# Position-wise-key attention: scores of two units at once in four row groups, and a new order on three engines

## The chip, the cores and the metric

The kernel runs on one NeuronCore of a Trainium2 chip. The time is the device time of one launch in microseconds (us). Engines are named as in the profile: PE is TensorE's matmul side, PEld its weight load, DVE is VectorE, ACT is ScalarE, POOL is GpSimd. Each engine works its own instructions strictly in the order in which the program lists them, and the engines wait for each other through counting semaphores.

## What is computed

The reference is a decoder of four layers over x (8 rows of 128 tokens, 256 features). The change lies in the self attention of the last layer (`_L3_attn_ref`), whose core is:

```python
x = x + _L3_attn_ref(_layernorm(x), Wq, bq, Wk, bk, Wv, bv, Wo, bo)
H, G = 32, 8; HPG = H // G; HD = 8          # 32 query heads, 8 key heads, 8 features each
q = q.reshape(b, n, H, HD).transpose(0, 2, 1, 3).reshape(b, G, HPG, n, HD)
k = k.reshape(b, n, G, HD).transpose(0, 2, 1, 3)
attn_prob = softmax(einsum('bghnd,bgsd->bghns', q, k) / sqrt(8), axis=-1)
out = einsum('bghns,bgsd->bghnd', attn_prob, v)   # then the product with Wo, plus bo
```

Everything is float32. Before this block comes the feed-forward block of layer 2 (names `L2f_`), behind it the linear cross attention of layer 3 (`L3x_`) and its feed-forward block (`L3f_`).

## The kernel before

**Units.** The block works through the 8 batch rows n. A row has 32 heads, cut into four units of 8 heads, so there are 32 units p = 4n + s. A unit's scores are a tile of 128 queries by 8 x 128 keys (`L3a_S[p % 2]`, two PSUM banks). `L3a_scores(p)` makes it with two matmuls, each over one group of 32 rows of the PE array (`r = 32 * (2 * s % 4 + u)`), with 512 columns; the two matmuls of a unit lie in two different row groups. A unit with even s uses row groups 0 and 1, one with odd s groups 2 and 3, and a half row of heads (c = 0 or 1) is two units.

**A unit's way.** DVE takes the maximum of the scores (`L3a_max`, L3173) and subtracts it into `L3a_P[p % 2]` (`L3a_sub`, L3179); ACT takes the exponential in place (`L3a_exp`, L2032); PE transposes the eight 128 x 128 blocks into the one PSUM tile `L3a_pT` (`L3a_pTr`, L4373); ACT copies that to `L3a_PT[p % 2]` (`L3a_pTc`, L2038). For each two units (a half b = 2n + c) PE multiplies with the values (`L3a_pv`, L4389: four matmuls in four column groups of 32, written to the PSUM bank `L3a_front`), ACT copies (`L3a_oTc`, L2044), PE transposes back into `L3a_oq` (`L3a_oTr`, L4406), and DVE divides by the sum (`L3a_norm`, L3186 and L3190). A row then has `L3a_aoTr` (L4416), the ACT copy `L3a_aoTc` (L2050), `L3a_project` (L4423) and on DVE `L3a_resid` (L3195).

**A row's front.** For the row that comes next: DVE `L3a_stats` and `L3a_u` (L3061), PE `L3a_uTr` (L4260), ACT `L3a_unT`, PE `L3a_value` (L4282) with DVE `L3a_values` (L3075), PE `L3a_qk` (q in L4269, k in L4272, eight matmuls), ACT `L3a_qTc` (L1969, two of them) and DVE `L3a_keys` (L3068, two of them: the keys plus bias, masked for each of four heads, into `L3a_kR`).

**Buffers that are shared.** `L3a_front` is one PSUM bank, used in turn by `uTr`, `qk`, `pv` and `aoTr`, each of which waits until the one before has been copied out. `L3a_oq`, `L3a_v` and `L3a_out` share another bank: `L3a_oTr` therefore waits for `L3a_resid` of the row whose projection lies there. `L3a_pT` is single: a `pTr` waits for the `pTc` before it. `L3a_S`, `L3a_P` and `L3a_PT` are double.

**Order.** Three loops over `p in range(38)`, written out by hand for PE, DVE and ACT, say which of these steps comes when. On PE, scores(p) comes first in each p, and pTr(p - 1) later; scores(p) waits for sub(p - 2), so one unit's scores can be made while DVE still reads those of the unit before.

Of the kernel before, what the change touches and what calls it, by code (L numbers as in the profile page):

```python
# [108 lines left out]
def build_program(nc, dram, out_d):  # L109
# [89 lines left out]
    with stack:  # L199
# [331 lines left out]
        cat = view(sbuf, 45128, [4, 128])  # L531
# [852 lines left out]
        def _(act):  # L1384
# [710 lines left out]

            for p in range(38):
                n, s = p // 4, p % 4
                if 2 <= p < 34:
                    L3a_pTc(p - 2)
                if s == 0 and n < 7:  # L2100
                    L3a_unT(n + 1)
                if s == 2 and n < 7:
                    L3a_qTc(n + 1)
                if s == 3 and n > 0:
                    L3a_aoTc(n - 1)
                if 3 <= p < 34 and p % 2 == 1:
                    L3a_oTc(p // 2 - 1)
                if p < 32:
                    L3a_exp(p)
                if s == 1 and n < 6:  # L2110
                    L3a_rstd(n + 2)
                if p in (29, 30, 31):
                    L3x_rstd(p - 29)
                if p == 32:
                    L3x_kexp(0)
                    L3x_vcopy(0)
                    L3x_unTc(0)
                if p == 34:
                    L3x_qexp(0)
                    L3x_gexp(0)  # L2120
                    L3x_gln(0)
                if p == 35:
                    L3x_kexp(1)
                    L3x_vcopy(1)
                    L3x_unTc(1)
# [112 lines left out]
        def _(dve):  # L2238
# [1005 lines left out]

            for p in range(38):
                n, s = p // 4, p % 4
                if p < 32:
                    L3a_max(p)
                    L3a_sub(p)
                if p == 0:  # L3250
                    L3a_u(1)
                if p == 1:
                    L2f_resid(7)
                if s == 0 and n < 6:
                    L3a_stats(n + 2)
                if s == 1 and n < 7:
                    L3a_values(n + 1)
                if s == 1 and n > 1:
                    L3a_resid(n - 2)
                if 4 <= p < 35 and p % 2 == 0:  # L3260
                    L3a_norm(p // 2 - 2)
                if s == 2 and n < 7:
                    L3a_keys(n + 1)
                if s == 2 and n < 6:
                    L3a_u(n + 2)
                if p == 27:
                    for a in range(2):
                        dve.memset(L3x_v[a][:, :, 128:256], 1.0)
                if p in (28, 29, 30):
                    L3x_stats(p - 28)  # L3270
                if p == 32:
                    L3x_kmin(0)
                if p == 33:
                    L3x_kmap(0)
                    L3x_qmin(0)
                if p == 34:
                    L3x_blocks(0)
                    L3x_qmap(0)
                if p == 35:
                    L3x_kmin(1)  # L3280
                    L3x_kmap(1)

            def L3f_stats(n):
# [119 lines left out]
        def _(pe):  # L3403
# [849 lines left out]
            def L3a_uTr(n):  # L4253
                pe.wait_ge(u_done, L3a_start['u'] + n + 1)
                if n == 1:
                    pe.wait_ge(kTc_done, L3a_start['kTc'] + 1)
                if n > 1:
                    pe.wait_ge(oTc_done, 2 * n - 3)
                for c in range(2):
                    last = pe.transpose(L3a_front[:, 128 * c:128 * c + 128], u0[:, 128 * c:128 * c + 128], ident[:, :])  # L4260
                last.then_inc(uT_done, 1)

            def L3a_qk(n):
                pe.wait_ge(unT_done, L3a_start['unT'] + n + 1)
                if n > 1:
                    pe.wait_ge(oTc_done, 2 * n - 2)
                for j in range(2):
                    for c in range(2):
                        pe.matmul(L3a_front[:, 128 * j:128 * j + 128], w_q3[:, c, 128 * j:128 * j + 128], unT0[:, c, :], start=c == 0, stop=c == 1)  # L4269
                for j in range(2):  # L4270
                    for c in range(2):
                        last = pe.matmul(L3a_front[:, 256 + 128 * j:384 + 128 * j], w_kr3[:, c, 128 * j:128 * j + 128], unT0[:, c, :], start=c == 0, stop=c == 1)  # L4272
                last.then_inc(q_done, 1)

            def L3a_value(n):
                if n > 0:
                    pe.wait_ge(unT_done, L3a_start['unT'] + n + 1)
                    pe.wait_ge(vc_done, L3a_start['vc'] + n)
                if n > 1:
                    pe.wait_ge(norm_done, L3a_start['norm'] + 2 * n - 3)  # L4280
                for c in range(2):
                    last = pe.matmul(L3a_v[:, :], unT0[:, c, :], w_v3[:, c, :], start=c == 0, stop=c == 1)  # L4282
                last.then_inc(v_done, 1)

            def L3a_scores(p):
                n, s = p // 4, p % 4
# [105 lines left out]
            def L3a_oTr(b):  # L4392
# [95 lines left out]
            pe.wait_ge(prod_done, L2f_start['prod'] + 96)  # L4488
            for p in range(38):
                n, s = p // 4, p % 4  # L4490
                if p < 32:
                    L3a_scores(p)
                if p == 0:
                    pe.wait_ge(vc_done, L3a_start['vc'] + 1)
                    L2f_out(7, 0)
                if p == 1:
                    L2f_out(7, 1)
                    pe.wait_ge(resid_done, L2f_start['resid'] + 8)
                if s == 0 and n < 7:
                    L3a_uTr(n + 1)  # L4500
                if 4 <= p < 35 and p % 2 == 0:
                    L3a_oTr(p // 2 - 2)
                if s == 1 and n > 1:
                    L3a_project(n - 2)
                if s == 1 and n < 7:
                    L3a_value(n + 1)
                if s == 2 and n < 7:
                    L3a_qk(n + 1)
                if s == 3 and n > 0:
                    L3a_aoTr(n - 1)  # L4510
                if p == 32:
                    L3x_context(0)
                    L3x_uTr(0)
                if 1 <= p < 33:
                    L3a_pTr(p - 1)
                if p == 33:
                    L3x_qgate(0)
                if 3 <= p < 34 and p % 2 == 1:
                    L3a_pv(p // 2 - 1)
                if p == 33:  # L4520
                    L3x_summary(0)
                if p == 34:
                    L3x_context(1)
                if p == 35:
                    L3x_uTr(1)

            def L3f_uTr(n):
# [290 lines left out]
```

## Time and profile before

| | |
|---|---|
| time, median of 3 | 2115.22 us (2112.89 to 2116.41) |
| the profiled execution: first to last instruction (its span) | 2108.1 us |
| median less that span | 7.1 us |
| first and last score matmul of the block's 32 units start at | 1723.8 and 1855.9 us |
| one period (one row, four units), from unit 8 to unit 28 | 16.29 us |
| busy over the whole span: PE, DVE, ACT, POOL | 87%, 70%, 51%, 52% |
| mean granted TensorE clock | 0.944 of full |

The profile gives only the span of its execution; what the device time counts around the span isn't in it. The block has a steady part, in which each row of four units takes the same 16.29 us, with a start before it (the last products of the block before are mixed in) and an end behind it (the cross attention's first steps are mixed in).

### The profile page before, as it was taken

Reading aid. Unit: us, or ns where it says so; the run is one execution under the profiler, and the core shown is the slowest. Engines: PE = TensorE matmul, PEld = TensorE weight load, DVE = VectorE, ACT = ScalarE, POOL = GpSimd, SP = SyncE. Lnnn points to the kernel's source line nnn. Section 1 sums busy time; section 2 is a strip of 40 time slices with the busy share of each in tenths; the row PEclk is TensorE's granted clock in tenths of the full one; section 3 lists DMA queues with packets and bytes.
Section 4 is the critical chain, followed back from the end, with each engine's and each line's share of the span. In section 5 each row is a group of like instructions: output and inputs, shape, how many; then the busy total and the mean of one; then the engine's idle time right before and its main releaser. Section 6 shows DMA issues by size and latency. Waiting matters only on the chain.

```text
span 2108.1 us, 31396 instructions
## 1 busy us (share of the span) xinstructions
PE 1839.7 (87%) x11498; PEld 1375.0 (65%) x11498; DVE 1485.6 (70%) x2499; ACT 1072.9 (51%) x2328; POOL 1089.3 (52%) x797
## 2 busy tenths in 40 slices
PE   7577779789899987899999999968888789998999
PEld 6111148545689965677777777757777665567887
DVE  5688962466764476677777777589999978866554
ACT  4444431334322254666666666556767656655443
POOL 2599950111692065555555555499999940023321
PEclk9689899689899998999999999989999989999999
DMA  4211001130400000110000000000000001000000
GB/s 162 49 35 35 0 1 40 38 160 0 181 1 1 1 21 21 51 34 1 1 1 1 1 1 17 36 8 1 1 1 1 26 9 74 1 1 1 6 9 9
DMA packets 22177, 54.88 MB, mean 26 GB/s; under 512 B 8591, under 2 KB 13752, under 8 KB 19592
## 3 DMA queue, kind: packets, MB, share of 16 engines
q1 hardware_dynamic: 22024, 52.88, 7.5%
q8 instruction: 92, 1.51, 0.3%
q14 instruction: 61, 0.50, 0.1%
HBM read 44.48 MB, written 1.05 MB: 22 GB/s over the span
## 4 chain that ended last, share of the span: by engine, by line
PE 53%; DVE 19%; POOL 12%; issue 8%; ACT 7%; SPq 1%; DMA 0%; DVEq 0%; POOLq 0%; ACTq 0%
POOL sbuf L1310 5%; PE psum L4153 4%; DVE sbuf L2309 3%; PE psum L4216 3%; PE psum L3507 2%; POOL sbuf L1318 2%; DVE psum L3120 2%; PE psum L4619 1%; POOL sbuf L1111 1%; PE psum L4185 1%; PE psum L4201 1%; PE psum L4157 1%; PE psum L4165 1%; PE psum L4313 1%; ACT sbuf L1893 1%
## 5 line engine op out<-in xcount | busy, mean ns | idle before, releaser
L1310 POOL TENSOR_TENSOR sbuf<-sbuf 128x1035 f32<-128x1035 f32 x128 | 248.4, 1969 | 0.9 <-ACT sbuf L1952 0.9
L4313 PE MATMUL psum<-sbuf 128*128 128x128 f32 (+1 forms) x1024 | 145.3, 292 | 58.4 <-ACT sbuf L1979 42.9
L1979 ACT ACTIVATE sbuf<-sbuf 128x1001 f32<-128x1001 f32 (+1 forms) x128 | 141.9, 1139 | 95.7 <-DVE sbuf L3128 62.9
L4313 PEld LDWEIGHTS psum<-sbuf 128*128 128x128 f32 (+1 forms) x1024 | 126.4, 153 | 79.4 <-ACT sbuf L1979 59.7
L1265 POOL TENSOR_TENSOR sbuf<-sbuf 128x512 f32<-128x512 f32 x64 | 66.7, 1042 | 187.7 <-DVE sbuf L2992 187.7
L1111 POOL TENSOR_TENSOR sbuf<-sbuf 128x1024 f32<-128x1024 f32 x64 | 149.9, 2356 | 16.9 <-DVE sbuf L2309 16.9
L2309 DVE TENSOR_TENSOR_SCAN sbuf<-psum,sbuf 128x1024 f32<-128x1024 f32 x64 | 144.7, 2278 | 12.5 <-ACT psum L1439 6.2
L3455 PE MATMUL psum<-sbuf 96*128 96x512 bf16 x256 | 83.5, 437 | 76.0 <-DVE sbuf L2309 32.7
L1893 ACT ACTIVATE sbuf<-psum,sbuf 128x128 f32<-128x128 f32 x256 | 90.4, 365 | 107.3 <-DVE sbuf L2986 107.3
L1439 ACT ACTIVATE psum<-psum,sbuf 128x1016 f32<-128x1016 f32 x64 | 69.0, 1081 | 125.7 <-PE psum L3455 125.7
L3120 DVE SCALAR_TENSOR_TENSOR psum<-sbuf,psum 128x1024 f32<-128x1024 f32 (+1 forms) x96 | 122.3, 1274 | 9.8 <-PE psum L4303 2.5
L4153 PE MATMUL psum<-sbuf 128*128 128x512 f32 x256 | 123.9, 607 | 3.5 <-POOL sbuf L1261 3.5
L3128 DVE TENSOR_TENSOR sbuf<-psum,sbuf 128x1024 f32<-128x1024 f32 (+1 forms) x96 | 116.4, 1213 | 3.3
L3455 PEld LDWEIGHTS psum<-sbuf 96*128 96x128 bf16 x256 | 18.7, 103 | 153.1 <-DVE sbuf L2309 63.4
L4216 PE MATMUL psum<-sbuf 128*128 128x256 bf16 x768 | 94.6, 273 | 14.5 <-POOL sbuf L1273 14.2
L1271 POOL TENSOR_TENSOR sbuf<-sbuf 128x512 f32<-128x512 bf16 x64 | 74.5, 1164 | 49.7 <-DVE sbuf L3005 48.1
L4216 PEld LDWEIGHTS psum<-sbuf 128*128 128x128 bf16 x768 | 71.3, 98 | 39.9 <-POOL sbuf L1273 30.7
L1363 POOL TENSOR_TENSOR sbuf<-sbuf 128x1024 f32<-128x1024 f32 x16 | 30.8, 1944 | 120.1 <-DVE sbuf L3321 120.1
L2981 DVE TENSOR_TENSOR sbuf<-psum,sbuf 128x512 f32<-128x512 f32 x64 | 44.3, 692 | 57.0 <-ACT sbuf L1877 57.0
L1273 POOL TENSOR_TENSOR sbuf<-sbuf 128x512 bf16<-128x512 f32 x64 | 81.2, 1268 | 5.0
L3486 PE MATMUL psum<-sbuf 128*32 128x512 f32 x256 | 77.6, 738 | 3.9 <-POOL sbuf L1111 3.9
L1099 POOL TENSOR_TENSOR sbuf<-sbuf 128x1024 f32<-128x1024 f32 x22 | 52.2, 2372 | 53.4 <-ACT sbuf L1445 53.4
(808 smaller groups left out, 5105.5 us busy)
## 6 DMA issues: line engine op xcount, KB each, us to landing
sbuf<-sbuf SPq DMA_DIRECT2D x42, 128.0 KB, 2.4
sbuf<-w_p_d SPq DMA_DIRECT2D x8, 512.0 KB, 3.7
sbuf<-w_qkv_d SPq DMA_DIRECT2D x3, 768.0 KB, 4.2
sbuf<-w_e_d SPq DMA_DIRECT2D x1, 2048.0 KB, 7.8
sbuf<-w_gu_d SPq DMA_DIRECT2D x1, 2048.0 KB, 9.0
sbuf<-w_gu_d SPq DMA_DIRECT2D x2, 1024.0 KB, 7.8
sbuf<-w_dn_d SPq DMA_DIRECT2D x1, 2048.0 KB, 15.8
sbuf<-w_q_d SPq DMA_DIRECT2D x1, 2048.0 KB, 8.3
```

The lines of the kernel that those rows point to most:

```text
L1111: pool.tensor_tensor(L0a_hc[i % 4][:, :], L0a_hs[i % 2][:, :], L0a_Cr[g % 4][:, :], ALU.mult).then_inc(hc_done, 1)
L1273: pool.tensor_tensor(cat16[:, :, :], cat[:, :, :], omagic[:, :, :], ALU.subtract).then_inc(cat_done, 1)
L1310: pool.tensor_tensor(P_r[g % 7][:, :, :], rows.unsqueeze(2).to_broadcast([128, 23, 45]), cols.unsqueeze(1).to_broadcast([128, 23, 45]), AL ...
L1893: last = act.activation(prob[:, h, :], L2x_s[:, h, :], ACT.Exp, bias=smax[:, h:h + 1], accum_out=esum[:, h:h + 1])
L1979: act.activation(Q_r[g % 6][:, 0:w], Q_r[g % 6][:, 0:w], ACT.Silu, scale=q8_p[n % 2][:, h:h + 1]).then_inc(silu_done, 1)
L2309: dve.tensor_tensor_scan(L0a_hs[i % 2][:, :], L0a_dAf[i % 2][:, :], L0a_us[i % 3][:, :], 0.0, ALU.mult, ALU.add).then_inc(scan_done, 1)
L3120: dve.scalar_tensor_tensor(M[:, 0:w], Pf_r[g % 7][:, o:o + w], t8_p[n % 2][:, h, 7:8], zps[:, 0:w], ALU.is_ge, ALU.mult).then_inc(mask_don ...
L3128: dve.tensor_tensor(Q_r[g % 6][:, 0:w], Mps[:, 0:w], Pf_r[g % 7][:, o:o + w], ALU.mult).then_inc(prod_done, 1)
L3455: last = pe.matmul(out[:, 512 * h:512 * h + 512], rows, L0a_stack[g % 4][0:96, a, 512 * h:512 * h + 512], start=True, stop=True)
L4153: last = pe.matmul(L2x_q[:, :, :], xs[:, vq, c, :], wq[:, c, 512 * g:512 * g + 512], start=c == 0, stop=c == 1)
L4216: last = pe.matmul(L2x_out[:, :], cat16[:, h, :], w_p3[p][:, 4 * (i % 8) + h, :], start=i % 8 == 0 and h == 0 and p == 0, stop=i % 8 == 7 ...
L4313: last = pe.matmul(Gps[0:m, c, :], Q_r[g % 6][:, 128 * c:128 * c + m], ident[:, :], start=h == 0 and c % 4 == 0, stop=h == 7, skip_group_c ...
```

## The change

The score step takes two units: `L3a_scores(k, units)` issues four matmuls, one in each row group, into both halves of `L3a_S`, and adds one to `score_done` behind each unit's two. It waits for both subtractions of the pair before. The loops run over 19 pair steps k instead of 38 units, and all steps on PE, DVE and ACT are laid into a new order, with the waits that this order needs. Number and shapes of all instructions stay as they are; no buffer is added. POOL's list doesn't change.

```diff
             def L3a_uTr(n):
-                if n == 1:
-                    pe.wait_ge(kTc_done, L3a_start['kTc'] + 1)
-                if n > 1:
-                    pe.wait_ge(oTc_done, 2 * n - 3)
+                if 0 < n < 3:
+                    pe.wait_ge(kTc_done, L3a_start['kTc'] + n)
+                if n > 2:
+                    pe.wait_ge(oTc_done, 2 * n - 4)
...
             def L3a_qk(n):
                 pe.wait_ge(unT_done, L3a_start['unT'] + n + 1)
                 if n > 1:
-                    pe.wait_ge(oTc_done, 2 * n - 2)
+                    pe.wait_ge(oTc_done, 2 * n - 3)
+                if n > 2:
+                    pe.wait_ge(cat_done, L3a_start['cat'] + n - 2)
...
             def L3a_value(n):
-                if n > 1:
-                    pe.wait_ge(norm_done, L3a_start['norm'] + 2 * n - 3)
+                if n > 2:
+                    pe.wait_ge(norm_done, L3a_start['norm'] + 2 * n - 4)
+                if n > 3:
+                    pe.wait_ge(resid_done, L3a_start['resid'] + n - 3)
...
-            def L3a_scores(p):
-                n, s = p // 4, p % 4
+            def L3a_scores(k, units):
+                n, c = k // 2, k % 2
                 pe.wait_ge(kTc_done, L3a_start['kTc'] + n + 1)
-                if p > 1:
-                    pe.wait_ge(sub_done, L3a_start['sub'] + p - 1)
-
-                for u in range(2):
-                    r = 32 * (2 * s % 4 + u)
-                    last = pe.matmul(L3a_S[p % 2][:, 4 * u:4 * u + 4, :], L3a_qT[n % 2][r:r + 32, s // 2, :], L3a_kR[n % 2][r:r + 32, s // 2, :, :], start=True, stop=True)
-
-                last.then_inc(score_done, 1)
+                if k > 0:
+                    pe.wait_ge(sub_done, L3a_start['sub'] + 2 * k)
+                for v in units:
+                    for u in range(2):
+                        r = 32 * (2 * v + u)
+                        last = pe.matmul(L3a_S[v][:, 4 * u:4 * u + 4, :], L3a_qT[n % 2][r:r + 32, c, :], L3a_kR[n % 2][r:r + 32, c, :, :], start=True, stop=True)
+                    last.then_inc(score_done, 1)
...
             def L3a_pv(b):
-                if c == 0 and n < 7:
-                    pe.wait_ge(kTc_done, L3a_start['kTc'] + n + 2)
-                if c == 0 and n > 0:
+                if c == 0 and n < 6:
+                    pe.wait_ge(unT_done, L3a_start['unT'] + n + 3)
+                if c == 1 and n < 6:
+                    pe.wait_ge(kTc_done, L3a_start['kTc'] + n + 3)
+                if c == 1 and n > 0:
                     pe.wait_ge(cat_done, L3a_start['cat'] + n)
-                if c == 1 and n < 6:
-                    pe.wait_ge(unT_done, L3a_start['unT'] + n + 3)
...
             def L3a_oTr(b):
                 if c == 0:
-                    pe.wait_ge(vc_done, L3a_start['vc'] + min(n + 2, 8))
-                if c == 0 and n > 1:
-                    pe.wait_ge(resid_done, L3a_start['resid'] + n - 1)
-                if c == 1:
                     pe.wait_ge(vc_done, L3a_start['vc'] + min(n + 3, 8))
                 if c == 1 and n > 0:
                     pe.wait_ge(resid_done, L3a_start['resid'] + n)
...
             def L3a_aoTr(n):
                 pe.wait_ge(norm_done, L3a_start['norm'] + 2 * n + 2)
-                if n < 6:
-                    pe.wait_ge(kTc_done, L3a_start['kTc'] + n + 3)
-                else:
-                    pe.wait_ge(oTc_done, 2 * n + 2)
+                pe.wait_ge(oTc_done, min(2 * n + 3, 16))
...
             def L3a_project(n):
+                if n < 6:
+                    pe.wait_ge(vc_done, L3a_start['vc'] + min(n + 4, 8))
```

The PE loop after the change (what steps 16 to 18 hold of the cross attention is left out):

```diff
+            for k in range(19):
+                if k == 0:
+                    L3a_scores(0, (0,))
+                    pe.wait_ge(vc_done, L3a_start['vc'] + 1)
+                    L2f_out(7, 0)
+                    L3a_uTr(1)
+                    L3a_scores(0, (1,))
+                    L2f_out(7, 1)
+                    pe.wait_ge(resid_done, L2f_start['resid'] + 8)
+                elif k < 16:
+                    L3a_scores(k, (0, 1))
+                if 1 <= k < 17:
+                    L3a_pTr(2 * k - 2)
+                if 2 <= k < 18:
+                    L3a_pv(k - 2)
+                if k % 2 == 0:
+                    if k < 14:
+                        L3a_value(k // 2 + 1)
...
+                    if k >= 4:
+                        L3a_aoTr(k // 2 - 2)
+                else:
+                    if k >= 5:
+                        L3a_project(k // 2 - 2)
+                    if k < 12:
+                        L3a_uTr(k // 2 + 2)
+                if 2 <= k < 18:
+                    L3a_oTr(k - 2)
+                if 1 <= k < 17:
+                    L3a_pTr(2 * k - 1)
+                if k % 2 == 0 and k < 14:
+                    L3a_qk(k // 2 + 1)
```

The DVE order of step k is now: norm(k - 3), max(2k), sub(2k); with even k then values(k/2 + 1) and u(k/2 + 2), with odd k from 5 on resid((k - 1)/2 - 2); then max(2k + 1), sub(2k + 1); then keys(k/2 + 1) with even k, stats with odd k. The ACT order of step k is: oTc(k - 2), pTc(2k - 2), aoTc (even k) or unT (odd k), exp(2k), pTc(2k - 1), qTc (even k), exp(2k + 1), rstd (odd k). From step 16 on the three loops hold the first steps of the cross attention, as before.

## Rows read from the trace of the kernel before

**Rows 1.** Windows: us, then busy us (and count) of PE, PEld, DVE, ACT, POOL; clock
```profile
1762.00:1843.40 81.40, 75.75 (x504) 46.05 (x500) 66.03 (x94) 51.64 (x78) 2.91 (x4) 1.00 0.00 1
1843.40:1872.40 29.00, 24.99 (x149) 14.68 (x145) 18.02 (x35) 17.56 (x32) 4.38 (x4) 1.00 0.00 1
```

**Rows 2.** Waits, 1774.5 to 1839.7 (four periods): us in total, times, longest
```profile
DVE sbuf L3173 <- PE psum L4293: 11.3, 12, 1.5
```

**Rows 3.** Timeline of one period: start us, us, engine, line, tile, count
```profile
1785.73 0.41 DVE L3195 TENSOR_TENSOR sbuf<-psum,sbuf 128x256 f32<-128x256 f32 x1
...
1787.48 0.66 PE L4406 MATMUL psum<-sbuf 128*128 128x128 f32 x4
...
1787.98 1.06 PE L4269 MATMUL psum<-sbuf 128*128 128x128 f32 x8
...
1788.86 1.22 DVE L3179 TENSOR_TENSOR sbuf<-psum,sbuf 128x1024 f32<-128x1024 f32 x1
1788.87 1.06 PE L4272 MATMUL psum<-sbuf 128*128 128x128 f32 x8
...
1789.77 1.04 PE L4373 MATMUL psum<-sbuf 128*128 128x128 f32 x8
1789.97 0.62 ACT L1969 ACTIVATE sbuf<-psum,sbuf 128x128 f32<-128x128 f32 x2 [0.53 <-PE psum L4272]
1790.00 0.25 DVE L3186 RECIPROCAL sbuf<-psum 128x16 f32<-128x16 f32 x1
1790.29 0.29 DVE L3190 TENSOR_TENSOR sbuf<-psum,sbuf 128x128 f32<-128x128 f32 x1
...
1790.62 1.41 DVE L3068 SCALAR_TENSOR_TENSOR sbuf<-psum,sbuf 128x512 f32<-128x512 f32 x2
...
1791.95 0.40 DVE L3061 TENSOR_SCALAR sbuf<-sbuf 128x256 f32<-128x256 f32 x1
...
1792.27 1.22 DVE L3173 TENSOR_REDUCE sbuf<-psum 128x8 f32<-128x1024 f32 x1
...
1793.52 1.23 DVE L3179 TENSOR_TENSOR sbuf<-psum,sbuf 128x1024 f32<-128x1024 f32 x1
...
1793.59 1.06 PE L4389 MATMUL psum<-sbuf 128*32 128x512 f32 x8
...
1794.59 1.13 PE L4293 MATMUL psum<-sbuf 32*128 32x512 f32 x4
1794.72 0.60 ACT L2044 ACTIVATE sbuf<-psum 128x512 f32<-128x512 f32 x1 [1.71 <-PE psum L4389]
1795.21 1.05 ACT L2032 ACTIVATE sbuf<-sbuf 128x1024 f32<-128x1024 f32 x1
...
1796.16 1.01 ACT L2038 ACTIVATE sbuf<-psum 128x1024 f32<-128x1024 f32 x1
...
1797.32 1.06 PE L4373 MATMUL psum<-sbuf 128*128 128x128 f32 x8 [0.80 <-ACT sbuf L2038]
```

**Rows 4.** Timeline, PE, next block's scores in four row groups
```profile
1920.32 1.15 PE L4559 MATMUL psum<-sbuf 32*128 32x256 f32 x16
```

**Rows 5.** Timeline, PE: value of unit 1, then units 8 and 28
```profile
1736.79 0.66 PE L4282 MATMUL psum<-sbuf 128*128 128x64 f32 x4 [0.52 <-DVE sbuf L3132]
...
1762.00 1.13 PE L4293 MATMUL psum<-sbuf 32*128 32x512 f32 x4
...
1843.44 1.13 PE L4293 MATMUL psum<-sbuf 32*128 32x512 f32 x4
```

**Rows 6.** Timeline, PE: third context product of the cross attention
```profile
1872.37 1.98 PE L4433 MATMUL psum<-sbuf 128*128 128x512 f32 x4
```

**Rows 7.** Windows around a fall of the clock (columns as in rows 1)
```profile
1715.80:1722.60 6.80, 3.46 (x28) 2.91 (x27) 5.18 (x6) 3.39 (x3) 1.61 (x2) 1.00 0.01 1
1722.60:1729.40 6.80, 6.80 (x19) 4.33 (x18) 3.35 (x5) 2.93 (x6) 0.57 (x1) 0.50 0.01 2
```

**Rows 8.** Timeline, PE: the first unit's scores at the low clock
```profile
1723.83 2.08 PE L4293 MATMUL psum<-sbuf 32*128 32x512 f32 x4
```

More of the change, by code:

```diff
@@ L2094, in L3x_rexp @@
                 act.activation(L3x_r[n % 2][:, :, :], L3x_r[n % 2][:, :, :], ACT.Exp, scale=-1.0).then_inc(factor_done, 1)
-            for p in range(38):
-                n, s = p // 4, p % 4
[L2098 to L2114, printed above, removed]
+            for k in range(19):
+                if k == 0:
+                    L3a_exp(0)
+                    L3a_unT(1)
+                    L3a_exp(1)
+                    L3a_qTc(1)
+                    L3a_rstd(2)
+                if 2 <= k < 18:
+                    L3a_oTc(k - 2)
+                if 1 <= k < 17:
+                    L3a_pTc(2 * k - 2)
+                if k % 2 == 0 and k >= 4:
+                    L3a_aoTc(k // 2 - 2)
+                if k % 2 == 1 and k < 12:
+                    L3a_unT(k // 2 + 2)
+                if k == 16:
+                    L3x_unTc(0)
+                if 0 < k < 16:
+                    L3a_exp(2 * k)
+                if 1 <= k < 17:
+                    L3a_pTc(2 * k - 1)
+                if k % 2 == 0 and 0 < k < 14:
+                    L3a_qTc(k // 2 + 1)
+                if 0 < k < 16:
+                    L3a_exp(2 * k + 1)
+                if k % 2 == 1 and k < 11:
+                    L3a_rstd(k // 2 + 3)
+                if k == 14:
+                    L3x_rstd(0)
+                if k == 15:
+                    L3x_rstd(1)
+                    L3x_rstd(2)
+                if k == 16:
                     L3x_kexp(0)
                     L3x_vcopy(0)
-                    L3x_unTc(0)
-                if p == 34:
+                if k == 17:
                     L3x_qexp(0)
@@ L3243, in L3x_resid @@
                 dve.tensor_tensor(x[:, n, :], L3x_O[:, :], x[:, n, :], ALU.add).then_inc(resid_done, 1)
[L3245 to L3250, printed above, removed]
-                    L3a_u(1)
-                if p == 1:
-                    L2f_resid(7)
[L3254 to L3266, printed above, removed]
+            for k in range(19):
+                if k == 1:
+                    L3a_u(2)
+                if k >= 3:
+                    L3a_norm(k - 3)
+                if k < 16:
+                    L3a_max(2 * k)
+                    L3a_sub(2 * k)
+                if k == 0:
+                    L3a_u(1)
+                if k % 2 == 0 and 0 < k < 12:
+                    L3a_values(k // 2 + 1)
+                    L3a_u(k // 2 + 2)
+                if k == 12:
+                    L3a_values(7)
+                if k % 2 == 1 and k >= 5:
+                    L3a_resid(k // 2 - 2)
+                if k < 16:
+                    L3a_max(2 * k + 1)
+                    L3a_sub(2 * k + 1)
+                if k == 0:
+                    L2f_resid(7)
+                    L3a_stats(2)
+                    L3a_values(1)
+                if k % 2 == 0 and k < 14:
+                    L3a_keys(k // 2 + 1)
+                if k % 2 == 1 and k < 11:
+                    L3a_stats(k // 2 + 3)
+                if k == 13:
@@ L3267, in _ @@
                     for a in range(2):
                         dve.memset(L3x_v[a][:, :, 128:256], 1.0)
[L3269 to L3271 removed]
+                if k == 14:
+                    L3x_stats(0)
+                if k == 15:
+                    L3x_stats(1)
+                    L3x_stats(2)
+                if k == 16:
                     L3x_kmin(0)
[L3273 removed]
                     L3x_kmap(0)
+                if k == 17:
@@ L4488, in _ @@
             pe.wait_ge(prod_done, L2f_start['prod'] + 96)
[L4489 to L4493, printed above, removed]
+            for k in range(19):
+                if k == 0:
+                    L3a_scores(0, (0,))
                     pe.wait_ge(vc_done, L3a_start['vc'] + 1)
                     L2f_out(7, 0)
-                if p == 1:
+                    L3a_uTr(1)
+                    L3a_scores(0, (1,))
@@ L4517, in _ @@
+                if 2 <= k < 18:
+                    L3a_oTr(k - 2)
+                if 1 <= k < 17:
+                    L3a_pTr(2 * k - 1)
+                if k % 2 == 0 and k < 14:
+                    L3a_qk(k // 2 + 1)
+                if k == 16:
                     L3x_qgate(0)
-                if 3 <= p < 34 and p % 2 == 1:
-                    L3a_pv(p // 2 - 1)
-                if p == 33:
+                if k == 17:
                     L3x_summary(0)
-                if p == 34:
                     L3x_context(1)
-                if p == 35:
+                if k == 18:
```

30 lines of the change are left out of this document (8 added, 22 removed).

## Prediction, made before the changed kernel was run

> **What bounds the kernel now.** I read the windows of the block first, then the waits in its steady part, then the timeline of one period. From unit 8 to unit 28 the same row of four units repeats five times: their scores start at 1762.00 and 1843.44 [rows 5], so a period is 81.44/5 = 16.29 us. In this stretch PE is busy 75.75 of 81.40 us, DVE 66.03, ACT 51.64 [rows 1]: 93%, 81% and 63%. DVE's largest wait is its maximum waiting for the scores, 11.3 us in four periods [rows 2]. So PE's list sets the pace, and one row costs PE about 15.2 and DVE about 13.2 us of work. PE alone would let the period fall with every matmul taken away; DVE's 13.2 is the next floor.
>
> **What the score matmuls cost.** A unit's two matmuls occupy PE for 1.05 us, from their start at 1794.59 to their end less the overlap with what follows, and their result is there 1.13 us after the start [rows 3]. The four value matmuls, in four column groups and of the same 512 columns, take 1.06 us together and let the scores start 1.00 us after their own start [rows 3]. The scores of the next block use all four row groups: 8 matmuls of 256 columns in 1.15 us [rows 4], which is the same number of columns for each row group as four matmuls of 512. So I cost the pair at 1.06 us of PE time where two units cost 2.11, with bounds of 1.00 (the value matmuls) and 1.15. One row has two pairs: PE gets back 2 x 1.05 = 2.1 us, and its work falls to about 13.1 us a period, just below DVE's 13.2. Whether this arrives is decided by the order and the waits.
>
> The Trainium skill, "TensorEngine Tiling (Array Packing)", Theoretical Speedup, gives up to 4x for a contraction of at most 32; its PSUM Bottleneck section says that after such a speedup the evacuation of PSUM may become the limit. The row of the four row groups agrees with the first; the first rule alone would give the 2.1 us a period in full, the second says that DVE's two passes over the scores take over.
>
> **What the change adds.** The pair's scores wait for both subtractions of the pair before. Before, one unit's scores were made while DVE read the other's. Now DVE must finish, then PE starts, then 1.17 us later the next maximum can begin. Behind the waiting scores on PE stands everything else of the step. I follow one period from T, the start of the scores of an even step k, all prices from [rows 3].
>
> *Even half, PE and ACT.* Scores 1.06; pTr 0.97 (from 1789.77 to the next matmul, as it overlaps what follows by 0.07); pv starts at 2.03 and ends at 3.10. value is issued behind it, but aoTr, oTr and the second pTr need ACT: oTc starts 0.07 later (3.17), ACT's next step, pTc of the first unit, 0.49 after that (3.66), and ends at 4.67; PE resumes 0.15 later (1796.16 + 1.01 to 1797.32) with the second pTr at 4.82. It lasts 0.97 (5.79), the eight qk matmuls 1.95 (1787.98 to 1789.93), so 7.74. qTc starts 0.04 later and takes 0.62, keys start 0.03 after that, at 8.43, and release DVE's next step 1.33 later (1790.62 to 1791.95): 9.76.
>
> *The same half on DVE.* Maximum from 1.17, subtraction, values, u, maximum, and the second subtraction, which must wait until the second pTr has emptied its buffer (4.82 + 1.06) and ends at about 7.14. Then DVE stands before keys until 8.43: 1.3 us idle that the period before doesn't have, because qk is now the last PE step of a 7.7 us half and keys come right behind the subtraction. The odd step's scores start at 7.6 and are ready before DVE is.
>
> *Odd half.* norm 0.50 (0.29 to the multiply, and that less 0.08 of overlap): 10.26. Maximum 1.26, subtraction 1.14 to the next: 12.66. resid takes 0.41: 13.07. oTr of this step waits for that residual, since both lie in one PSUM bank; PE's earlier steps (pv behind the keys at about 10.0, project, uTr) are done at 12.3, so PE stands idle. I allow 0.10 from DVE to PE, between 0.06 and 0.15. oTr 0.50, pTr 1.04: 14.71, and only then may the fourth subtraction write its buffer: 14.75, otherwise 14.25. It takes 1.22, 15.97, and 0.10 later the next pair's scores start: **T' = 16.07 us**, against 16.29. So of 2.1 us taken from PE, 0.2 arrive; the rest becomes waits of PE (about 0.6 in the even half, 0.4 before pv, 0.8 before oTr, 1.4 before the next scores). Bounds for the period: 15.9 (scores 1.00, both hand-overs 0.06) and 16.3 (1.15 and 0.15).
>
> **The start.** PE's list is the same up to value of row 1 at 1736.79 [rows 5]. qk follows about 0.50 later: 1737.29, +1.95 +0.04 +0.62 +0.03 = 1739.93, keys 1.33, u 0.32 (1791.95 to 1792.27), maximum 1.26, subtraction 1.14, maximum 1.26, subtraction 1.22 and 0.10: units 4 and 5 start at 1746.56. The next period has no projection or residual: 10.26 + 1.26 + 1.14 + 1.26 + 1.22 + 0.10 = 15.24, so unit 8 starts at 1761.80, 0.2 earlier than now. Five periods gain 5 x 0.22 = 1.1 more, with bounds of 0 and 2: unit 28 starts at about 1842.1 instead of 1843.44.
>
> **The end.** From there to the third context product of the cross attention the kernel now needs 1872.37 - 1843.44 = 28.93 us [rows 5, 6], PE busy 24.99 of it [rows 1]. The pair order lags by one pTr and one pv more at that point, 0.97 + 1.00, and saves 2 x 1.05: 24.9. Its waits, counted as above: in step 14, 0.6 for oTc and pTc and 1.4 for the scores (the second subtraction is held until 5.92, so step 15 starts at 7.24, PE is free at 5.8); in step 15, 0.7 for the residual and 1.3 for pTc of unit 29, behind which step 16 starts; in steps 17 and 18 another 0.7 and 0.3 for the last residuals and copies. That is 5.0, together 29.9, so 1.0 us is given back here (I allow 1 us either way).
>
> **The sum.** -0.2 - 1.1 + 1.0 = -0.3 us on the profiled execution of 2108.1, which is 2107.8; the median lies 7.1 above that span, so 2114.9. Work outside the block isn't touched, and no DMA moves.
>
> **Rivals.** *DVE becomes the only bound (faster).* If qk and keys don't hold DVE, as when PE runs through the even half faster than my chain, the period is DVE's 13.2 to 13.4 plus 0.3 for the score hand-over of the even step: 13.7, and five periods save 5 x 2.6 = 13 us: about 2102. For: the busy shares [rows 1]. Against: every link of the chain is a row, and keys can't precede qk. Half of it, say keys held by 0.6 less and the residual by nothing, gives 5 x 1.1 = 5.5 us: 2109. Losing the residual's hold alone is 5 x 0.5 = 2.4 us, still within the noise. It decides from 0.8 us a period on.
>
> *The clock falls (slower).* At 1722.6 the granted clock went to the half level (1.2 of 2.4 GHz) after PE had been busy 3.46 of 6.80 us, and stayed there for 6.8 us of full work [rows 7]; the scores took 2.08 instead of 1.13 us in it [rows 8]. In the steady part with 93% it never fell. After the change PE does about 1.5 us of work in the 3.7 us between uTr and the next scores, some 40%, once in each period, though 80% over all. One fall for a few us, right where the next even half begins, costs about 0.95 on the scores, 0.6 on pTr: 1.5 us. One such fall gives 2116.4; from three on (2119.4) the change is slower beyond what can be measured; a fall in every one of the five periods gives 2122.4.
> The Trainium skill, "TensorE: Matmul & The Clock Gate", section on the HAM clock gate, says that the throttled state is the default and activity releases it. By that alone idle PE time isn't free; the fall in the trace agrees, but no stretch there looks like the new odd half.
>
> *The change doesn't do what it says (slower).* If the four matmuls run two at a time, the pair costs 2.11. The chain grows by 1.05 in the even half and by some 0.15 in the odd: 5 x 1.2, and some 2 at start and end: 2123. Against it stand the 16 records in 1.15 us [rows 4].
>
> **How the numbers follow.** My forecast, gains of the PE time turned into waits: 0.55. DVE-bound or on the way there: 0.25. Clock: 0.14. No concurrency: 0.06. About 0.2% (4.2 us) is what a measurement of this kernel can tell from no change. The forecast with one or two falls of the clock stays inside it: same 0.55; faster 0.25; slower 0.20. The forecast's own range is 2112 to 2118 (period 15.9 to 16.3, the end 1 us either way, one or two falls, the scatter of the median). The whole range is 2108.5 to 2120.5: it holds the half of the DVE case that is near, and the clock case up to three or four falls; beyond lie some 0.12 and 0.08.
>
> **What would show it.** Right: score matmuls eight records in about 1.15 us, starting 0.1 after a subtraction in odd-to-even steps; a period of 15.9 to 16.3; PE busy near 80% and DVE near 82% in it; DVE's longest wait now before keys (L3068) instead of before the maximum, about 1.3 us a period; PE waiting for the residual before L4406's matmuls in odd steps; the full clock throughout. Wrong: a period under 15.5, which would mean that keys come earlier than 8.4 us after T, or the half clock in the steady part, or scores of over 2 us.

## The result

| | median | lowest to highest | runs |
|---|---|---|---|
| kernel before | 2114.42 us | 2109.21 to 2116.64 | 20 |
| kernel changed | 2117.76 us | 2111.10 to 2124.34 | 20 |

The ratio of the times is 1.0018, with a 95% interval of 1.0011 to 1.0025: the change makes the kernel 2.3 to 5.3 us slower, a little under the 0.2% that I had called measurable. I had forecast 0.3 us less. The sign is wrong and the size is small. The 2117.76 us still lie inside my range of 2112 to 2118, which had room for one or two falls of the clock; the direction is what failed.

The profile after: the span is 2115.7 us, and its own run took 2117.47, so only 1.8 us lie around a span, and not the 7.1 that I had worked out. The 2108.1 us of before was a quick execution, and its span can't be compared with the 2115.7 as a whole: the first score matmul starts at 1728.90 instead of 1723.83, in work that the change doesn't touch. What I compare is the stretch from the first score to the third context product of the cross attention, in three parts, read from the starts of the score and context matmuls in each timeline:

| kernel, trace | start: first score to unit 8 | five periods, units 8 to 28 | end: unit 28 to context | sum | half clock inside it, from (for) |
|---|---|---|---|---|---|
| before, profile shown above | 38.17 | 81.44 | 28.93 | 148.54 | 1722.6 (6.8, into the start) |
| before, second trace | 35.77 | 81.44 | 28.92 | 146.13 | none |
| changed | 40.02 | 80.88 | 30.34 | 151.24 | 1729.9 (3.4), 1750.4 (6.8) |
| changed, second trace | 37.47 | 80.87 | 30.36 | 148.70 | 1745.7 (3.4) |
| changed, third trace | 39.80 | 80.90 | 30.36 | 151.06 | 1727.1 (6.8, into the start), 1751.0 (3.4) |

The two second traces enter the block alike, with the full clock, so they are the fair pair: +1.70 us in the start, -0.57 in the five periods, +1.44 in the end, together +2.57, within the interval of the timing. The first trace before and the third changed one also enter alike, both at the half clock, and differ by +1.63, -0.54, +1.43, together +2.52. Outside the stretch executions of one kernel differ more than that: 2108.1 - 148.54 = 1959.6 us in one trace of the kernel before and 2110.6 - 146.13 = 1964.5 in the other.

The windows of the profile after, for the five periods and the end (columns as in [rows 1]: us, then busy us and count of PE, PEld, DVE, ACT, POOL, then the clock):

```profile
1768.90:1849.80 80.90, 66.72 (x499) 43.77 (x499) 65.29 (x93) 52.08 (x78) 2.91 (x4) 1.00 0.00 1
1849.80:1880.10 30.30, 25.11 (x162) 15.33 (x162) 18.21 (x37) 18.40 (x33) 4.38 (x4) 1.00 0.00 1
```

Against [rows 1] PE is busy 66.72 of 80.90 us instead of 75.75 of 81.40: nine microseconds of PE work are gone from five periods, and half a microsecond of time. The waits in four of the periods (us in total, times, longest):

```profile
PE psum L4320 <- DVE sbuf L3192: 5.9, 4, 1.5
DVE sbuf L3192 <- PE psum L4399: 5.2, 8, 0.9
DVE sbuf L3081 <- ACT sbuf L1969: 4.6, 4, 1.2
...
PE psum L4428 <- DVE sbuf L3208: 3.2, 4, 0.8
...
DVE sbuf L3186 <- PE psum L4320: 1.7, 4, 0.8
```

The maximum's wait for the scores, 11.3 us in [rows 2], is down to 1.7. In its place stand PE before the pair's scores (5.9), the subtractions behind pTr (5.2), keys behind qTc (4.6) and oTr behind the residual (3.2): the waits that the prediction listed. One period of the timeline (start, duration, engine, line; DVE's lines lie 13, PE's 19 to 27 higher than in the kernel before, and differ by a few more in the experiments):

```profile
1785.10 1.14 PE L4320 MATMUL psum<-sbuf 32*128 32x512 f32 x8 [1.48 <-DVE sbuf L3192]
...
1788.82 1.02 ACT L2038 ACTIVATE sbuf<-psum 128x1024 f32<-128x1024 f32 x1
...
1789.98 1.06 PE L4399 MATMUL psum<-sbuf 128*128 128x128 f32 x8
...
1791.77 1.06 PE L4297 MATMUL psum<-sbuf 128*128 128x128 f32 x8
...
1792.76 1.14 PE L4320 MATMUL psum<-sbuf 32*128 32x512 f32 x8
...
1793.53 1.41 DVE L3081 SCALAR_TENSOR_TENSOR sbuf<-psum,sbuf 128x512 f32<-128x512 f32 x2 [1.15 <-ACT sbuf L1969]
...
1797.73 0.41 DVE L3208 TENSOR_TENSOR sbuf<-psum,sbuf 128x256 f32<-128x256 f32 x1
...
1798.29 0.63 PE L4428 MATMUL psum<-sbuf 128*128 128x128 f32 x4 [0.80 <-DVE sbuf L3208]
...
1798.76 1.04 PE L4399 MATMUL psum<-sbuf 128*128 128x128 f32 x8
...
1799.90 1.22 DVE L3192 TENSOR_TENSOR sbuf<-psum,sbuf 128x1024 f32<-128x1024 f32 x1 [0.62 <-PE psum L4399]
...
1801.27 1.14 PE L4320 MATMUL psum<-sbuf 32*128 32x512 f32 x8 [1.48 <-DVE sbuf L3192]
```

From T = 1785.10: pTc at 3.72, the second pTr at 4.88, the end of the k products at 7.73, keys at 8.43, resid at 12.63, oTr at 13.19, the fourth subtraction at 14.80, T' at 16.17. The eight records of the pair take 1.14 us. The prediction had 3.66, 4.82, 7.74, 8.43, 12.66, 13.17, 14.75 and 16.07.

The start is where it goes wrong. PE's rows of the changed kernel, and the windows over the idle stretch and over step 2:

```profile
1743.37 1.14 PE L4320 MATMUL psum<-sbuf 32*128 32x512 f32 x8
...
1746.74 1.06 PE L4399 MATMUL psum<-sbuf 128*128 128x128 f32 x8 [0.38 <-ACT sbuf L2038]
1750.80 2.09 PE L4320 MATMUL psum<-sbuf 32*128 32x512 f32 x8 [2.99 <-DVE sbuf L3192]
1752.82 1.97 PE L4399 MATMUL psum<-sbuf 128*128 128x128 f32 x8
```

```profile
1746.90:1750.40 3.50, 0.91 (x8) 0.67 (x7) 3.43 (x4) 1.97 (x2) 0.00 (x0) 1.00 0.98 410
1750.80:1761.16 10.36, 9.95 (x56) 6.20 (x56) 5.72 (x8) 4.81 (x7) 0.73 (x1) 0.69 0.24 95
```

PE waits 2.99 us for the fourth subtraction, is busy 0.91 of 3.50 us there, and the clock goes to its half level (1.2 GHz) for 6.8 us, with the scores of step 2 at 2.09 instead of 1.14 us. Step 2 takes 10.36 us. The kernel before has no such hole: it makes single units' scores there, while DVE reads the other buffer, and its longest PE wait between 1740 and 1755 is 0.80 us in both of its traces.

### The profile page after: what moved, and what is told of

Same layout as the page of the kernel before. It is cut to its first block, busy times and chain, and to the rows that moved or that the text cites. A ratio compares the mean times of both kernels' runs of the same rounds, so it can differ in the third digit from the quotient of the medians.

```text
span 2115.7 us, 31372 instructions
## 1 busy us (share of the span) xinstructions
PE 1832.4 (87%) x11498; PEld 1374.8 (65%) x11498; DVE 1486.0 (70%) x2499; ACT 1074.8 (51%) x2328; POOL 1089.1 (51%) x797
## 4 chain that ended last, share of the span: by engine, by line
PE 54%; DVE 20%; POOL 11%; issue 8%; ACT 7%; SPq 1%; DMA 0%; DVEq 0%; POOLq 0%; ACTq 0%
POOL sbuf L1310 4%; PE psum L4176 4%; DVE sbuf L2322 3%; PE psum L4239 3%; PE psum L3530 2%; DVE psum L3133 2%; POOL sbuf L1318 1%; POOL sbuf L1111 1%; PE psum L4339 1%; PE psum L4645 1%; PE psum L4208 1%; PE psum L4399 1%; PE psum L4224 1%; PE psum L4180 1%; PE psum L4188 1%
```

## The experiments

Ratios are to the kernel before, timed beside each on the same chip. "Sum" is the stretch of the table above, from the first score to the third context product.

**The trace once more, before and changed, unchanged.** These are the second traces of the table.

> The kernel before once more, unchanged, for a second trace: how much of the span outside the block, and of the block's start, differs from one execution to the next. From the first score to the third context product 148.5 us, plus or minus 1.5 by where the half clock of the block before ends; the periods 16.29; no half clock between unit 2 and unit 31.

> The changed kernel once more, unchanged. Theory A (the clock falls in the idle stretch of step 1 in nearly every run): a half clock of 3.4 us or more within 3 us of the scores of step 2; 150 to 151.5 us from the first score to the third context product; periods of 16.18. Theory B (chance): no fall there, 148.5 us.

The changed kernel's PE rows around step 2, then the scores of units 4, 6 and 8 of the kernel before:

```profile
1740.45 1.06 PE L4399 MATMUL psum<-sbuf 128*128 128x128 f32 x8 [0.38 <-ACT sbuf L2038]
1744.51 1.14 PE L4320 MATMUL psum<-sbuf 32*128 32x512 f32 x8 [2.99 <-DVE sbuf L3192]
1745.58 1.88 PE L4399 MATMUL psum<-sbuf 128*128 128x128 f32 x8
...
1753.81 1.14 PE L4320 MATMUL psum<-sbuf 32*128 32x512 f32 x8
...
1761.57 1.14 PE L4320 MATMUL psum<-sbuf 32*128 32x512 f32 x8 [1.48 <-DVE sbuf L3192]
```

```profile
1746.75 1.13 PE L4293 MATMUL psum<-sbuf 32*128 32x512 f32 x4
...
1754.55 1.13 PE L4293 MATMUL psum<-sbuf 32*128 32x512 f32 x4
...
1762.70 1.13 PE L4293 MATMUL psum<-sbuf 32*128 32x512 f32 x4
```

In the changed kernel the half clock comes again, for 3.4 us from 1745.7: pTr takes 1.88 us, and step 2 takes 1753.81 - 1744.51 = 9.30 instead of the 7.67 of later even steps. So the fall costs 1.63 us when it lasts 3.4 us, and 10.36 - 7.67 = 2.69 when it lasts 6.8. Without it this start would be 37.47 - 1.63 = 35.84, equal to the 35.77 of before. The sum fell below my 150 to 151.5 (148.70), because that range assumed a start partly at the low clock; for the same reason the kernel before gave 146.13, below my 147.

**Filling the hole.** To the changed kernel, 20 transposes of the identity are added on PE in step 1; nothing reads what they write.

```diff
+                if k == 1:
+                    pe.wait_ge(vc_done, L3a_start['vc'] + 2)
+                    for i in range(20):
+                        pe.transpose(L3a_oq[:, i % 4, :, :], ident[:, :], ident[:, :])
```

> The changed kernel plus 20 transposes of the identity on PE in step 1, written to the idle tile of the normalised outputs (values 1 have been read by then), between pTr(1) and the scores of step 2. In the changed kernel's trace PE is idle 2.99 us before those scores and the granted clock is at the half level from 1750.4 for 6.8 us. Theory A (the start costs what it does because the clock falls in that idle stretch, in nearly every run): no half clock between step 1 and step 3, the scores of step 2 to those of step 3 take about 7.7 us instead of 10.36, and the time falls by about 2.7 us against the changed kernel (2117.8), so about 2115 and a ratio of about 1.000 to before. Theory B (the fall is chance, the loss comes from the waits of the new order): the time stays at 2117 to 2118, ratio about 1.002.

> The changed kernel with the filling transposes once more, beside the changed kernel on the same chip. Theory A: 1.6 to 2.7 us faster than the changed kernel. Theory B: equal within 1 us. In the trace no half clock within 4 us of the scores of step 2.

> The changed kernel unchanged, timed beside e10: ratio to before about 1.0018 again, a half clock within 3 us of the scores of step 2, 150 to 151.5 us from the first score to the third context product where the block before leaves the same clock.

The last of these is the changed kernel's third trace in the table; its sum of 151.06 and its half clock at 1751.0, just before the scores of step 2 at 1751.12, are as expected. PE around step 2 with the filling:

```profile
1750.19 2.35 PE L4545 MATMUL psum<-sbuf 128*128 128x128 f32 x20
1753.34 1.14 PE L4320 MATMUL psum<-sbuf 32*128 32x512 f32 x8 [0.80 <-DVE sbuf L3192]
...
1761.00 1.14 PE L4320 MATMUL psum<-sbuf 32*128 32x512 f32 x8
```

The 20 transposes end 0.8 us before the scores, step 2 takes 1761.00 - 1753.34 = 7.66 us, and no half clock comes near it in either filled trace; the periods and the end are as in the changed kernel (80.88 and 30.35). The half clock came in all eight traces of pair-order kernels without filling, from 0.8 us before to 1.2 us after the start of the scores of step 2 (in those of the experiments below too), and in none of the four with it. PE's pause before those scores was 2.99 us in six of the eight, 3.26 with the keys first and 1.81 with the pair split; with filling it was 0.80 to 1.07. The second filled trace enters the block at the half clock as the first trace before does, and its start takes 38.23 us against 38.17: the fall is the whole loss of the start. In the time: the filled kernel 1.0013 (1.0000 to 1.0026), and a second time 1.0009 (0.9998 to 1.0020), beside the unfilled one with 1.0018 (1.0006 to 1.0031), 2112.90 against 2115.37 us. That is the direction and the size of theory A, but the intervals overlap; the traces show it, the timing alone doesn't. With the filling, what is left of the loss is the end less the periods: a sum of 149.48 us in that second filled trace against 148.54.

**Two row groups at a time.** The second unit's matmuls wait for the first's.

```diff
                 for v in units:
+                    if v == 1 and k > 0:
+                        pe.wait_ge(score_done, L3a_start['score'] + 2 * k + 1)
                     for u in range(2):
```

> The changed kernel with the second unit's two score matmuls waiting until the first unit's are done, so that only two row groups run at a time. Theory A (my chain: the pair's scores lie on the path in the even half, and use up slack of about 0.4 us in the odd half): the even half grows by about 1.2 us, the odd by 0.2 to 0.3, the period from 16.18 to about 17.6, the time by 8 to 10 us to about 2126 to 2128. Theory B (PE's score time is hidden behind DVE, which sets the pace): the period stays within 0.2 us and the time at about 2118.

2135.01 us, ratio 1.0109 (1.0089 to 1.0128): much more than either theory. Below are windows of one period at the full clock and of two periods before it, then the scores on PE, first those of step 2:

```profile
1828.80:1846.70 17.90, 15.55 (x100) 9.34 (x101) 13.31 (x20) 10.52 (x17) 0.72 (x1) 1.00 0.01 1
1766.70:1808.10 41.40, 37.12 (x200) 21.31 (x201) 26.64 (x39) 21.10 (x33) 1.46 (x2) 0.84 0.00 1
```

```profile
1746.42 3.26 PE L4322 MATMUL psum<-sbuf 32*128 32x512 f32 x8 [1.81 <-DVE sbuf L3192]
...
1828.82 2.31 PE L4322 MATMUL psum<-sbuf 32*128 32x512 f32 x8 [1.48 <-DVE sbuf L3192]
...
1837.66 2.32 PE L4322 MATMUL psum<-sbuf 32*128 32x512 f32 x8
...
1846.72 1.88 PE L4322 MATMUL psum<-sbuf 32*128 32x512 f32 x6 [1.48 <-DVE sbuf L3192]
```

At the full clock the pair takes 2.31 us, the even half 8.84 (+1.17) and the odd half 9.06 (+0.55), a period 17.90. That is theory A's chain, with more of the slack in the odd half used up than I had thought. The rest is the clock: it fell at step 2, from 1747.6, and then in the steady part from 1768.1, 1788.6 and 1809.1, each time for 6.8 us, and twice more in the end, from 1867.1 and 1877.3, for 3.4 us each. A period with a fall takes 1787.35 - 1766.73 = 20.62 us, 2.7 more. So making the four row groups' scores at once is worth 17.90 - 16.18 = 1.72 us a period even at the full clock. And neither the idle share nor the longest pause of PE says by itself whether the clock falls: here PE is idle for 17.90 - 15.55 = 2.35 us of a period at the full clock, less than the (80.90 - 66.72)/5 = 2.84 of the changed kernel, whose steady periods never lost it, and the pause before the pair's scores is 1.48 us in both.

**A third buffer for the probabilities.** `L3a_P` gets a third tile, `p % 3` in its users, and a subtraction waits for the pTr three units back:

```diff
-                if p > 1:
-                    dve.wait_ge(pT_done, L3a_start['pT'] + p - 1)
+                if p > 2:
+                    dve.wait_ge(pT_done, L3a_start['pT'] + p - 2)
```

> The changed kernel with a third buffer for the probabilities, so that a subtraction waits for the pTr three units back instead of two. Theory A (the odd half is held by residual, oTr, pTr, fourth subtraction): the fourth subtraction starts 0.6 us earlier, the period falls from 16.18 to about 15.6, the time by about 4 us against the changed kernel: about 2113.5. The even half's length doesn't change, since there keys wait for qTc anyway. Theory B (the wait of the subtraction only takes the place of another): period and time stay within 0.3 us and 1 us.

```profile
1786.93 1.14 PE L4320 MATMUL psum<-sbuf 32*128 32x512 f32 x8
...
1791.90 0.41 DVE L3208 TENSOR_TENSOR sbuf<-psum,sbuf 128x256 f32<-128x256 f32 x1
...
1792.92 1.04 PE L4399 MATMUL psum<-sbuf 128*128 128x128 f32 x8
1793.48 1.22 DVE L3192 TENSOR_TENSOR sbuf<-psum,sbuf 128x1024 f32<-128x1024 f32 x1
...
1794.85 1.14 PE L4320 MATMUL psum<-sbuf 32*128 32x512 f32 x8 [0.89 <-DVE sbuf L3192]
```

The fourth subtraction now starts at 1793.48, half a microsecond into the last pTr, without a wait; the even half is 7.67 as before, the odd half 7.92 instead of 8.51. Five periods take 77.95 us (15.59 each), the end 29.11 instead of 30.35. The sum is 144.36, 4.34 less than in the changed kernel's second trace. The time is 2109.63 us, ratio 0.9992 (0.9979 to 1.0006), about 0.26% less than the changed kernel's ratio. Theory A holds to a few hundredths in the trace. The end is then only 0.19 us longer than the 28.92 of the kernel before, so most of what the end gives back is this one wait too.

**pv ahead of the first pTr in even steps.**

```diff
-                if 1 <= k < 17:
+                if 1 <= k < 17 and (k % 2 == 1 or k == 16):
                     L3a_pTr(2 * k - 2)
                 if 2 <= k < 18:
                     L3a_pv(k - 2)
+                if 1 <= k < 16 and k % 2 == 0:
+                    L3a_pTr(2 * k - 2)
```

> The changed kernel with pv ahead of the first pTr in the even steps (order on PE only). Theory A (the even half is set by the chain pv, oTc, pTc, second pTr, qk, qTc, keys): the second pTr, qk and keys come 0.5 us earlier, the period falls to about 15.7, the time by about 3 us against the changed kernel: about 2114.5; the first subtraction is held 0.7 us by the later pTr, at no cost. Theory B (the even half is set by DVE): the held subtraction makes it longer by up to 0.7 us, about 2121.

```profile
1784.44 1.14 PE L4320 MATMUL psum<-sbuf 32*128 32x512 f32 x8 [1.48 <-DVE sbuf L3192]
...
1787.71 1.22 DVE L3192 TENSOR_TENSOR sbuf<-psum,sbuf 128x1024 f32<-128x1024 f32 x1 [0.88 <-PE psum L4399]
...
1788.85 0.21 DVE L3088 TENSOR_TENSOR sbuf<-psum,sbuf 128x64 f32<-128x64 f32 x1
...
1789.21 0.63 PE L4428 MATMUL psum<-sbuf 128*128 128x128 f32 x4 [0.99 <-DVE sbuf L3088]
...
1789.68 1.04 PE L4399 MATMUL psum<-sbuf 128*128 128x128 f32 x8
```

A miss: the period grew to 16.50, the even half to 7.99. Five periods took 82.50 us, the time is 2113.71 us, ratio 1.0005 (0.9992 to 1.0019). The first subtraction starts 3.27 us after the scores (1787.71) instead of 2.42, `values` comes right behind it on DVE at 1788.85, and oTr, which may not overwrite the bank before `values` has read it, waits 0.99 us for it. The second pTr starts at 5.24 instead of 4.88. The chain that I had named was shortened, and a second one, subtraction, values, oTr, took its place: I had checked what the subtraction's delay costs DVE, not who waits for the step behind it. (The timing doesn't show this: the sum of 152.50 is 1.4 us above that of the changed kernel's third trace, which would make a ratio of about 1.0025, outside the interval. Why is open.)

**Both together.**

> The third probability buffer and pv ahead of the first pTr in even steps, together. Alone, the second made the period longer (16.50 against 16.18), because the first subtraction was held by the later pTr, values stood behind it on DVE, and oTr waits for values. Theory A: with the third buffer that subtraction isn't held, values come at 3.6 us after the pair's scores again, the second pTr starts at about 4.45 instead of 4.89 us, the even half falls from 7.67 to about 7.2, the period to about 15.15, the time by about 2.5 us against the third buffer alone (2109.6): about 2107. Theory B (oTr and the second pTr stay late for another reason): the period stays at 15.6 or more, the time at 2109.6 or above.

```profile
1795.36 1.14 PE L4320 MATMUL psum<-sbuf 32*128 32x512 f32 x8 [0.89 <-DVE sbuf L3192]
...
1797.78 1.23 DVE L3192 TENSOR_TENSOR sbuf<-psum,sbuf 128x1024 f32<-128x1024 f32 x1
...
1799.79 1.04 PE L4399 MATMUL psum<-sbuf 128*128 128x128 f32 x8
...
1802.54 1.14 PE L4320 MATMUL psum<-sbuf 32*128 32x512 f32 x8
```

With the third buffer the subtraction isn't held, it starts 2.42 us after the scores as in the changed kernel, and the second pTr starts at 4.43. The period is 15.10 (75.52 for five), the even half 7.18. The time is 2104.18 us, ratio 0.9970 (0.9957 to 0.9982): the first version that beats the kernel before.

**Both, with the hole filled.**

> As e5, plus the filling transposes in step 1. Theory A: no half clock around step 2, another 1 to 3 us less than e5: about 2105, a ratio to before of 0.996 to 0.998. Theory B (filling does nothing that can be timed): equal to e5 within 1 us.

The sum falls from 141.43 to 139.78, the 1.65 us of the fall. The time doesn't: 2106.84 us, ratio 0.9976 (0.9966 to 0.9986), not lower than without filling. The two intervals overlap, and with 6 to 10 us between the quickest and the slowest run a difference of 1.65 us isn't resolved by 12 runs each.

**Keys before queries.** On top of both: DVE's keys wait for the k products directly, ACT's qTc waits for keys, and what waited for keys to free the bank waits for qTc.

```diff
             def L3a_qTc(n):
                 act.wait_ge(q_done, L3a_start['q'] + n + 1)
+                if n > 0:
+                    act.wait_ge(kTc_done, L3a_start['kTc'] + n + 1)
...
             def L3a_keys(n):
-                dve.wait_ge(qTc_done, L3a_start['qTc'] + n + 1)
+                if n > 0:
+                    dve.wait_ge(q_done, L3a_start['q'] + n + 1)
+                else:
+                    dve.wait_ge(qTc_done, L3a_start['qTc'] + n + 1)
```

> The kernel with the third buffer and pv first, and in addition the keys are copied by DVE before the queries are copied by ACT (both lie in one PSUM bank, so one must wait for the other; so far the queries went first). Theory A (the odd half begins when the keys are written: q, k, qTc, keys in a chain): keys start 0.65 us earlier, right behind the k products, the period falls from 15.1 to about 14.5, the time by about 3 us to about 2101, ratio about 0.9955. Theory B (DVE or another wait already bounds the odd half): the period stays within 0.2 us.

> The same with the filling transposes in step 1: no half clock near step 2, 1.6 us or more less than without in the block; in the time 1 to 3 us less if filling is worth what the traces of the block say, no difference if something outside the block eats it.

```profile
1806.05 1.14 PE L4329 MATMUL psum<-sbuf 32*128 32x512 f32 x8
1806.16 1.41 DVE L3086 SCALAR_TENSOR_TENSOR sbuf<-psum,sbuf 128x512 f32<-128x512 f32 x2 [0.76 <-PE psum L4304]
...
1809.48 1.13 PE L4453 MATMUL psum<-sbuf 128*128 128x256 f32 x4
...
1810.72 0.42 DVE L3213 TENSOR_TENSOR sbuf<-psum,sbuf 128x256 f32<-128x256 f32 x1 [0.27 <-PE psum L4453]
```

keys start 0.11 us behind the odd step's scores instead of 0.77, the 0.65 us as expected. But the period falls by 0.29 only, to 14.81, where I had expected 14.5: the residual now waits 0.27 us for the projection, which stands behind pv, and pv waits for the queries' copy, the later of the two now. The times are 2108.14 (ratio 0.9984, 0.9972 to 0.9996) and, filled, 2104.46 (0.9970, 0.9959 to 0.9981). The filled one is 3.7 us lower here, and its sum is 140.62 against 143.54; both enter the block at the half clock of the block before. By the traces the filled kernel with all three edits has the shortest periods; by the timing it and the one with two edits can't be told apart.

## Why the prediction was wrong

*The score matmuls* were sized rightly: 1.14 us for the pair's eight records, 1.07 to the next matmul, against 1.06.

*The period* was right in mechanism and nearly in size: 16.18 against 16.07 forecast and 16.29 before. Each wait that I named is there, and of the signs that I gave for being right only "the full clock throughout" failed. The term that was mis-sized is the hand-over from DVE to PE: 0.15 us before oTr and again before the scores, where I took 0.10, and 0.10 instead of 0.04 from pTr to the subtraction. Five periods gave 0.57 us instead of 1.1.

*The start* is the step that failed: "unit 8 starts at 1761.80, 0.2 earlier than now". In the fair pair it is 1.70 later. Up to step 2 the sum was right: 1746.56 - 1723.83 = 22.73 us forecast and 22.83 measured in the third changed trace, which enters the block as the first trace before does. The next period was forecast at 15.24 us and took 16.97; with the filling it takes 15.43, so its waits were right within 0.2 us and 1.54 are the fall of the clock (2.69 in the first changed trace). The sum followed keys, u, two maxima and two subtractions on DVE, and never asked what PE does meanwhile: in the rows it has finished at 1747.80 and starts again at 1750.80. The sum has no term for a fall of the clock there. The clock rival stood in the prediction with the right price for one fall (1.5 us; 1.54 and 1.63 measured for short ones and 2.69 for a long one), but at the wrong place, the odd half of the steady periods, where none fell in any trace of the changed kernel; and as a chance of 0.14, while in the start it came in every trace. [rows 7] showed the pattern: PE busy half of a stretch of 6.8 us, then the half clock.

*The end* was forecast at +1.0 and measured at +1.44, within the 1 us that I allowed. PE is busy 25.11 of 30.30 us, where I had 24.9 of 29.9; whether its waits are those of my list one by one isn't shown. With the third buffer the end takes 29.11.

*The sum* then is +1.70 - 0.57 + 1.44 = +2.57 where I had -0.2 - 1.1 + 1.0. *The absolute time* had an error besides: I took the difference of 7.1 us between median and span for what lies around a span. It is 1.8, and the rest is that executions of one kernel differ by some 7 us.

*The rival "DVE becomes the only bound"* didn't come, as keys, residual and pTr hold DVE. The three edits, one on top of the other (15.59, 15.10, 14.81 us a period), walk towards its 13.7. *No concurrency* is refuted by the rows, and its price of 8 us was too low: the split pair's period is 17.90 us at the full clock where that chain gives 16.07 + 1.2 = 17.27, and the falls of the clock come on top.

The Trainium skill, "TensorEngine Tiling (Array Packing)", PSUM Bottleneck, says that reading the scores out may become the limit once the matmuls run in tiles. This case agrees in part: DVE, which reads the scores out, is busy 65.29 of 80.90 us and so isn't full; what the freed PE time runs into is the ring of waits in which DVE's passes over the scores stand.

What stays open: how often and for how long the clock falls over many executions is known from eight unfilled traces, not from the timed runs, and the gain of the filling is resolved by the timing in none of the three pairs with and without it (lower by 2.47 and 3.68 us in two, higher by 2.66 in one, all within the scatter). Why the clock fell in the periods of the split pair and never in those of the changed kernel is open too.

## What to carry to other kernels

Taking work from the busiest engine pays only as far as the slowest ring of waits through all engines gets shorter: write the ring down for one period, with every hand-over between engines at its measured price (up to 0.15 us here), and price the ring, not the busy share. A batch of two that waited for both of its predecessors traded PE's work for PE's idle time here; look at the ramp-up steps as closely as at the steady ones, because there the hole was largest (3 us against 1.5), and a hole can cost TensorE's clock as well as its own length. When a step is delayed "at no cost", look at the step behind it on the same engine and ask who waits for that one.

## What was not expected of the hardware

In the changed kernel a single pause of 2.99 us on PE, with 0.91 us of matmuls in 3.50 us around it in the first trace, was followed by the half clock in all three traces, for 3.4 or 6.8 us, though PE was busy 82% over the periods that followed; in the five unfilled variants the same step lost the clock as well, behind a pause of 2.99 us in three of them, of 3.26 and of 1.81 in the others. With the score pair split, four falls came 20.5 us apart (1747.6, 1768.1, 1788.6, 1809.1), about the 20.62 us that a period with a fall takes, and then stopped for the rest of the steady part without any change in the work.
